# Attention inside a fused layer on one core: maxima from all parts of q and k, and a new order of TensorE's queue

## What is computed

```python
q = rope((x @ Wq.T + bq).reshape(B, L, H, hd))
k = rope((x @ Wk.T + bk).reshape(B, L, H, hd))
scores = einsum('bqhd,bkhd->bhqk', q, k) / sqrt(hd)
attn = softmax(scores)
out = einsum('bhqk,bkhd->bqhd', attn, v) @ Wo.T + bo
```

## Time and profile before

| | us |
|---|---|
| median of 3 runs | 5264.52 (5264.1 to 5265.49) |
| profiled execution | 5257.78 |
| its span, first to last instruction | 5255.9 |
| PE busy | 4717.2 (90%) |
| DVE busy | 3750.7 (71%) |
| POOL busy | 2560.1 (49%) |
| ACT busy | 2358.7 (45%) |

### The profile page before, as it was taken

One profiled execution on the slowest core, in us unless ns is written; L12 is line 12 of the kernel. 1 busy time (PEld: TensorE's weight loads), 2 busy tenths in 40 slices (PEclk: granted clock), 3 DMA queues, 4 the chain that ended last, 5 costly groups with the idle time before them and its releaser, 6 DMA issues. The chain is left out here.

```text
span 5255.9 us, 83572 instructions
## 1 busy us (share of the span) xinstructions
PE 4717.2 (90%) x25792; PEld 3011.7 (57%) x25792; DVE 3750.7 (71%) x5321; ACT 2358.7 (45%) x3683; POOL 2560.1 (49%) x1341
## 2 busy tenths in 40 slices
PE   6689999968888799999999999999996775999999
PEld 6678888846666433333333333333333664888888
DVE  6667777667787677777777777777774886677776
ACT  4433333322222255565656556565653343333332
POOL 2334444345565455555555555555554554344443
PEclk9999999989999799999999999999997886999999
DMA  4465555334444422222222232222214554555552
GB/s 136 139 198 179 172 176 161 119 135 159 153 144 140 133 51 64 63 64 64 64 58 57 63 64 64 62 64 64 64 37 129 169 160 139 177 178 168 173 175 91
DMA packets 431929, 613.85 MB, mean 117 GB/s; under 512 B 188288, under 2 KB 189568, under 8 KB 431808
## 3 DMA queue, kind: packets, MB, share of 16 engines
q1 hardware_dynamic: 390848, 545.67, 36.8%
q0 software_dynamic: 40960, 66.65, 4.0%
HBM read 452.44 MB, written 178.33 MB: 120 GB/s over the span
## 5 line engine op out<-in xcount | busy, mean ns | idle before, releaser
L1468 POOL TENSOR_TENSOR att_pairsum<-att_p,att_p 128x1024 f32<-128x1024 f32 x512 | 1203.1, 2369 | 994.5 <-ACT att_p L1486 994.5
L1540 DVE TENSOR_REDUCE att_halves<-att_mx 128x2 f32<-128x1024 f32 x1024 | 1211.2, 1221 | 534.3 <-PE att_mx L1579 531.1
L1486 ACT ACTIVATE att_p<-att_st 128x512 f32<-128x512 f32 x2048 | 1183.5, 597 | 869.1 <-PE att_st L1601 831.2
L1601 PE MATMUL att_st<-att_q,att_k 128*128 128x512 f32 x2048 | 960.3, 494 | 48.0 <-ACT att_p L1486 46.5
L1601 PEld LDWEIGHTS att_st<-att_q,att_k 128*128 128x128 f32 x2048 | 372.7, 187 | 825.7 <-issue 409.3
L1611 PE MATMUL att_op<-att_p,att_v 128*32 128x512 f32 x4096 | 549.0, 608 | 1.1 <-ACT att_p L1486 1.0
L1579 PE MATMUL att_mx<-att_k,att_q 32*128 32x512 f32 x2048 | 520.0, 503 | 27.7 <-DMA att_v<-v 15.1
L845 DVE TENSOR_TENSOR e_w<-e_raw,e_w 128x2048 fp32r<-128x2048 f32 x192 | 439.3, 2290 | 10.0 <-ACT e_w L840 6.1
L863 ACT ACTIVATE e_sg<-e_gp 128x324 f32<-128x324 f32 x256 | 113.3, 443 | 630.9 <-PE e_up L176 630.9
L840 ACT ACTIVATE e_w<-e_raw 128x2048 fp32r<-128x2048 f32 x192 | 366.4, 1909 | 56.1 <-DMA e_raw<-in_w_gate 48.1
L899 DVE SCALAR_TENSOR_TENSOR e_xg<-e_yp,e_meta,e_xg 108x512 f32<-108x512 f32 x192 | 144.2, 751 | 314.9 <-PE e_yp L176 314.9
(11 more groups left out here) (147 smaller groups left out, 9176.0 us busy)
## 6 DMA issues: line engine op xcount, KB each, us to landing
e_raw<-in_w_gate SPq DMA_DIRECT2D x64, 1024.0 KB, 5.6
e_raw<-in_w_up SPq DMA_DIRECT2D x64, 1024.0 KB, 9.5
e_raw<-in_w_down SPq DMA_DIRECT2D x64, 1024.0 KB, 5.8
att_q<-q SPq DMA_DIRECT2D x192, 256.0 KB, 4.1
att_k<-k SPq DMA_DIRECT2D x256, 128.0 KB, 5.8
r_x<-in_x SPq DMA_DIRECT2D x16, 1024.0 KB, 6.0
x<-r_base SPq DMA_DIRECT2D x16, 1024.0 KB, 9.4
qkv_x<-x SPq DMA_DIRECT2D x16, 1024.0 KB, 5.6
```

What stands on the lines that cost most here:

```text
L1468: nc.gpsimd.tensor_tensor(out=pairsum[h][g % 2][:, :], in0=pr[h][2 * g % RING][:, :], in1=pr[h][(2 * g + 1) % RING][:, :], op=ALU.add).the ...
L1486: nc.scalar.activation(pr[h][kt % RING][:, c * HALF:(c + 1) * HALF], st[c][:, :], ACT.Exp, scale=SCALE).then_inc(s_exp, 1)
L1540: nc.vector.tensor_reduce(out=halves[:, n // 2, n % 2, :], in_=mx[n % 2][:, :, :], axis=AX.X, op=ALU.max).then_inc(s_max, 1)
L1601: nc.tensor.matmul(st[c][:, :], kst[b][:, h, kt * P:(kt + 1) * P], qst[b][:, h, c * HALF:(c + 1) * HALF], start=True, stop=True).then_inc( ...
```

## The change

- `kst` is loaded as three blocks of both heads (parts 0, 1, 0), so `N_IN` is 7 and not 9.
- `rough` uses rows 0 to 96, all three terms of the product, one matmul for each head.
- Every step now has two roughs, one before each of its last two scores, and its first two scores follow each other. `TURN` is 3: from step 3 on the roughs are those of the pair after the next, ten of which are so made ahead (`FIRST` = 5 query tiles of two).
- The row is placed in step 4 (`ROW`) before the scores, into the bank of the sums `zp`, one 32-partition tile for each head and half. Each engine copies it in two halves.
- The totals of a pair's first two groups move from steps 4 and 6 to steps 5 and 6; the first waits for the copies of the row. `copy_z` moves from after score (3, 0) to after score (2, 2).
- DVE's split has two maxima of the same halves, one written in float32 and one in bfloat16, in place of a maximum and a cast. It comes after the reductions of step 2.

```diff
-    ROUGH = ((1, 1, 1), (1, 0, 1), (1, 1, 1), (1, 0, 1), (1, 1, 1), (0, 0, 0), (0, 0, 1), (1, 0, 1))
-    TURN = KT - 2
+    TURN = 3
+    ROW = TURN + 1
+    FIRST = KT - TURN
...
-                sp.dma_start(kst[b][2 * HD:3 * HD, :, :].bitcast(F32),
-                             k_in[0, src[0], :].rearrange("(h d) q -> d h q", h=2)).then_inc(s_in[b], 16)
-                for h in range(2):
-                    for blk in range(2):
-                        sp.dma_start(kst[b][blk * HD:(blk + 1) * HD, h, :].bitcast(F32),
-                                     k_in[KBLK[h][blk], bass.ds(p * (2 * HD) + h * HD, HD), :]).then_inc(s_in[b], 16)
+                for blk, part in enumerate((0, 1, 0)):
+                    sp.dma_start(kst[b][blk * HD:(blk + 1) * HD, :, :].bitcast(F32),
+                                 k_in[part, src[0], :].rearrange("(h d) q -> d h q", h=2)).then_inc(s_in[b], 16)
...
             def copy_row(i, b):
 
                 act.wait_ge(s_row, DEPTH * i + b + 1)
-                nc.scalar.activation(qst[b][3 * HD:4 * HD, 1, :],
-                                     mx[1][2 * HD:3 * HD, :, :].rearrange("p c q -> p (c q)"),
-                                     ACT.Copy).then_inc(s_rowq[1], 1)
+                for c in range(2):
+                    nc.scalar.activation(qst[b][3 * HD:4 * HD, 1, half(c)], zp[tile(1, c), :],
+                                         ACT.Copy).then_inc(s_rowq[1], 1)
...
-                        if last and (kt, x) == (3, 0):
+                        if last and (kt, x) == (2, 2):
                             copy_z(*last)
-                        if left and (kt, x) == (TURN, 3):
+                        if left and (kt, x) == (ROW, 2):
                             copy_row(*ahead(i, b, 1))
...
+            def split(i, b):
+
+                p = DEPTH * i + b
+                dve.wait_ge(s_max, 2 * KT * (p + 1))
+                dve.wait_ge(s_mlo, p)
+                nc.vector.tensor_tensor(out=big[:, :, :], in0=halves[:, 0, :, :], in1=halves[:, 1, :, :],
                                         op=ALU.max).then_inc(s_big, 1)
-                dve.wait_ge(s_big, p + 1)
-                nc.vector.tensor_copy(parts[:, :, :, 0], big[:, :, :]).then_inc(s_mhi, 1)
-                dve.wait_ge(s_mhi, p + 1)
+                dve.wait_ge(s_row, p)
+                nc.vector.tensor_tensor(out=parts[:, :, :, 0], in0=halves[:, 0, :, :], in1=halves[:, 1, :, :],
+                                        op=ALU.max).then_inc(s_big, 1)
+                dve.wait_ge(s_big, 2 * (p + 1))
                 nc.vector.tensor_tensor(out=parts[:, :, :, 1], in0=big[:, :, :], in1=parts[:, :, :, 0],
                                         op=ALU.subtract).then_inc(s_mlo, 1)
...
             def step(i, b, left):
                 if left:
-                    maxima(*ahead(i, b, 1))
-
-            maxima(0, 0)
+                    for qt in range(FIRST, KT):
+                        maxima(*ahead(i, b, 1), qt)
+                    split(*ahead(i, b, 1))
+                for qt in range(FIRST):
+                    if left >= 2:
+                        maxima(*ahead(i, b, 2), qt)
+                    if left and qt == ROW - TURN - 1:
+                        copy_row(*ahead(i, b, 1))
...
+                for h in range(2):
+                    last = nc.tensor.matmul(mx[c][:, h, :], qst[b][0:3 * HD, h, qt * P:(qt + 1) * P],
+                                            kst[b][0:3 * HD, h, half(c)], start=True, stop=True)
+                last.then_inc(s_mx, 1)
+
+            def row(i, b):
+
+                p = DEPTH * i + b
+                pe.wait_ge(s_mlo, p + 1)
+                pe.wait_ge(s_zo, past(p - 1))
+                for t in range(KT // 2):
                     for h in range(2):
...
+                        for c in range(2):
+                            last = nc.tensor.matmul(zp[tile(h, c), t * P:(t + 1) * P], parts[:, h, c * (KT // 2) + t, :],
+                                                    identb[:, :], start=True, stop=True)
                 last.then_inc(s_row, 1)
...
-                    if kt in (4, 6):
-                        totals(p, kt // 2 - 2)
-                    if kt == TURN:
-                        n = 0
-                    for part in range(4):
-                        if part < 2:
-                            scores(p, b, kt, 2 + part)
-                        elif kt + 1 < KT:
-                            scores(p, b, kt + 1, part - 2)
+                        totals(p - 1, 2 + kt // 2, left)
+                    if kt == ROW and left:
+                        row(*nxt)
+                    if kt in (ROW + 1, ROW + 2):
+                        totals(p, kt - ROW - 1, left)
+                    for x in (2, 3):
+                        scores(p, b, kt, x)
+                    for x in (0, 1):
+                        if kt < TURN and left:
+                            rough(*nxt, FIRST + kt, x)
+                        if kt >= TURN and left >= 2:
+                            rough(*ahead(i, b, 2), kt - TURN, x)
+                        if kt + 1 < KT:
+                            scores(p, b, kt + 1, x)
                         elif left:
-                            scores(p + 1, nxt[1], 0, part - 2)
...
+                            scores(p + 1, nxt[1], 0, x)
```

More of the change, by code:

```diff
@@ L1397, in attention, with tile, half @@
         N_OUT = 4
-        N_IN = 3 + 5 + 1
-        KBLK = ((0, 1, 0), (1, 0, 0))
+        N_IN = 3 + 3 + 1
+        def tile(h, c):
+            return slice((2 * h + c) * HD, (2 * h + c + 1) * HD)
+        def half(c):
+            return slice(c * HALF, (c + 1) * HALF)
         def ahead(i, b, k):
@@ L1533, in _, with maxima @@
             nc.vector.tensor_copy(identb[:, :], ident[:, :]).then_inc(s_identb, 1)
-            def maxima(i, b):
+            def maxima(i, b, qt):
                 p = DEPTH * i + b
[L1538 to L1544, removed]
+                for c in range(2):
+                    dve.wait_ge(s_mx, 2 * (KT * p + qt) + c + 1)
+                    if qt == 0 and c == 0:
+                        dve.wait_ge(s_big, 2 * p)
+                    nc.vector.tensor_reduce(out=halves[:, c, :, qt], in_=mx[c][:, :, :], axis=AX.X,
+                                            op=ALU.max).then_inc(s_max, 1)
@@ L1560, in _ @@
+            for qt in range(KT):
+                maxima(0, 0, qt)
+            split(0, 0)
+            copy_row(0, 0)
+            for qt in range(FIRST):
+                maxima(0, 1, qt)
             rounds_by(DEPTH, dve, NP, step)
@@ L1566, in _, with rough @@
             pe.wait_ge(s_identb, 1)
-            def rough(i, b, n):
+            def rough(i, b, qt, c):
                 p = DEPTH * i + b
-                qt, c = n // 2, n % 2
-                if n == 0:
+                if qt == 0 and c == 0:
                     pe.wait_ge(s_in[b], 16 * N_IN * (i + 1))
[L1574 to L1577, removed]
+                pe.wait_ge(s_max, past(2 * (KT * p + qt) + c - 1))
                 for h in range(2):
-                    last = nc.tensor.matmul(mx[n % 2][:, h, :], qst[b][h * HD:(h + 1) * HD, h, qt * P:(qt + 1) * P],
-                                            kst[b][h * HD:(h + 1) * HD, h, c * HALF:(c + 1) * HALF],
-                                            start=True, stop=True)
+                    last = nc.tensor.matmul(mx[c][:, h, :], qst[b][0:3 * HD, h, qt * P:(qt + 1) * P],
+                                            kst[b][0:3 * HD, h, half(c)], start=True, stop=True)
                 last.then_inc(s_mx, 1)
@@ L1586, in row @@
                 p = DEPTH * i + b
-                pe.wait_ge(s_max, NM * (p + 1))
                 pe.wait_ge(s_mlo, p + 1)
-                for qt in range(KT):
+                pe.wait_ge(s_zo, past(p - 1))
+                for t in range(KT // 2):
                     for h in range(2):
-                        last = nc.tensor.matmul(
-                            mx[1][(3 - h) * HD:(4 - h) * HD, qt // (KT // 2), qt % (KT // 2) * P:(qt % (KT // 2) + 1) * P],
-                            parts[:, h, qt, :], identb[:, :], start=True, stop=True)
+                        for c in range(2):
+                            last = nc.tensor.matmul(zp[tile(h, c), t * P:(t + 1) * P], parts[:, h, c * (KT // 2) + t, :],
+                                                    identb[:, :], start=True, stop=True)
                 last.then_inc(s_row, 1)
@@ L1610, in products, with totals @@
                     for c in range(2):
-                        last = nc.tensor.matmul(op[(2 * h + c) * HD:(2 * h + c + 1) * HD, :], v[b][:, kt, h, :],
-                                                pr[h][kt % RING][:, c * HALF:(c + 1) * HALF],
+                        last = nc.tensor.matmul(op[tile(h, c), :], v[b][:, kt, h, :], pr[h][kt % RING][:, half(c)],
                                                 start=kt == 0, stop=kt == KT - 1)
                 last.then_inc(s_v, 1)
-            def totals(p, g):
```

(25 more changed lines are left out.)

24 lines of the change are left out of this document (10 added, 14 removed).

## The result

The changed kernel takes 5288.07 us (median of 7 runs, 5278.68 to 5293.52), the kernel before in the same measurement 5263.24 (7 runs): ratio 1.0047, 95% interval 1.0036 to 1.0059. It is slower by 0.47%, or 25 us; the forecast was 5290. Its profiled execution took 5291.72 us, with a span of 5289.8.

The account below looks back on a forecast made before the run. PE's queue was taken to set the period of 33.73 us. Longer periods (21 us) and prologue (8), less 1 for the last but one pair, gave 28 us over the median 5264.52, rounded down to 5290; range 5268 to 5325.

Parts of the forecast that it names:

- The slots: Each step, u from its first score: chained matmuls start 0.23 us apart; plain step 3.41, with totals 4.27, with copies 4.44.
- rival 3: In the steps: the stall stands but slots are shorter, 0.05 us a step; about 5267 us; chance 0.11.
- Rival 2: On PE, chained matmuls of different tiles cost 0.34 us each or more: 2.7 us a period, 5460 us; chance 0.12.
- Step 4: Before the row, PE waits 1.7 us for DVE's split, which needs both POOL sums over; step 6.42 us, period 34.07.
- rival 1: DVE's split gets SBUF before POOL, so the row goes 1.74 us earlier; period 32.33 us, 5185 us; chance 0.23.
- The main part: In the steady state, each period is 0.34 us longer than before: 21 us over 62 periods.
- The prologue: Before the first score, seven more roughs of pair 1 are reduced, 1.13 us each: 8 us, bounds 0 and 16.
- The first and the last pairs: In the last but one pair, five steps lack roughs and are 0.3 us shorter: -1 us in the sum.

Follow-up runs that it names:

- e3: The changed kernel with both maxima of the split made by a reduction of one SBUF input: 5145.83 us, ratio 0.9784 to the kernel before.
- e7: The changed kernel with two matmuls of no use put in front of the row's wait to keep PE busy: 5246.88 us, ratio 0.9976 to the kernel before.
- e4: The changed kernel with the old rough products of 32 rows and the old loads of k: 5425.71 us, ratio 1.0317 to the kernel before.
- e2: The changed kernel with the split one step later and the row in step 5: 5145.32 us, ratio 0.978 to the kernel before.

## Why the prediction was right, and where two of its terms were not

**The slots.** Confirmed to 0.02 us up to the last score: in the step at 2513.68 the rough comes at u = 0.57, the next score at 1.18, rough 1 at 1.52, the last score at 1.99. From there to the products I took 0.43, a change of shape; it measured 0.33. Steps are thus 3.31 to 3.32 and 4.17 us, not 3.41 and 4.27, except those with a copy on ACT, which sets their last score: 4.44 and 4.45, as forecast. This is rival 3's cause at 0.1 us a step. Rival 2 is out: the scores' and roughs' chain runs at 0.23.

**Step 4.** Right in mechanism and size. From the first score of step 2 (2525.60): POOL at 3.38 (forecast 3.46), the split at 3.65 (3.63), the row at 8.49 (8.62), the step 6.37 (6.42). The row to its next score took 0.34, not 0.45, and the last score waited 0.33 for ACT. From the start of step 4's products to the row it is 2.58 us (2.62), which the profile shows as 1.51 idle because it counts the products' drain as busy. The lead of POOL that rival 1 hung on is 0.27. Rival 1 was priced too small, too: had the split been fast, as in e3, the period would have been 31.93 and not 32.33, since the steps are shorter than I had them.

**The clock: the term that I left out.** I read the wait of 1.7 us before the row as 1.7 us and nothing more. It also brings a half-speed stretch soon after in more than half of the periods, 37 us by e7. My rows had a steady period at 1.00 with idle times up to 0.56 us, and the first pair at 0.50; none had an idle time of this length in a steady period, and I gave the step from the one to the other no bound, though the first pair shows what half clock is like.

**The sum.** The main part was forecast at +0.34 a period and measured 34.15 - 33.78 = +0.37, so +23 us and not +21; but it is the sum of two errors that nearly cancel, -0.42 a period for the shorter steps and row (33.65, e7's mean, against 34.07) and +0.50 for the dips. (The first hides no error of the mechanism: it is 0.1 in each of the five steps without ACT's copies and 0.05 in step 4, less about 0.1 for the longer periods that e7 has as well.) The prologue took 11 us more, not 8: from the first rough to the first score 24.2 us before and 35.2 after. The clock is 0.50 there, and with two matmuls of 96 rows to a rough the roughs come 1.27 us apart (four in 5.08), where they came 1.13 apart before: 7 more of them are 8.9, and the other 19 are dearer by 0.14 each, 2.7, about 11 in all. I had priced the seven at DVE's pace and the others at nothing. The first and the last pairs gave back 8 us, not 1. Together 26 us against 28. The forecast's closeness is so in part luck: without the dips 5250 would have been the result, faster than before by what e7 shows and below the forecast's own range (5268 to 5325), and my chance for a gain of that kind (0.25) was put on another mechanism.

**What stays open.** Why a dip lasts 3.4 us in one period and 6.8 in another, and why 21 of the 56 steady periods have none at the same idle time, no run here shows.

## What to carry to other kernels

An operation of 0.2 us on DVE can take 2 us beside POOL's adds: here a maximum of two inputs in SBUF did, and a cast of one, and a reduction did not. Look at when POOL reads, or try another form of the operation, before moving its consumer around. A reordering should be costed with the stall that it creates and with what the stall does to TensorE's clock afterwards: a dip is seen only in the windows after the wait, and filling the gap with two matmuls that nobody reads got 37 us back. And when the order of a queue is tuned, remove one wait and read again: stall (140 us), ACT's copies (103) and the place of one rough (82) came into view one after the other.

## What the hardware did that I had not expected

- The granted clock fell to 0.50 *after* PE had resumed from an idle time of 1.5 to 1.6 us, in steady periods of the changed kernel 1.1 to 1.5 us after, for 3.4 or 6.8 us, in 35 of 56. e4, with waits of 1.1 to 1.4 us there, had dips in 53 of 56. With waits of at most 0.58 us (before), 0.5 (e7) or 0.9 (e2) the clock stayed at 1.00 from 1900 to 3600 us.
- Eight more matmuls a pair took the instruction queue from 65 to 183 packets and stopped PE for 3.0 to 3.5 us once per four pairs; two more did neither.
- A cast with one input in SBUF waited for POOL's sums as a maximum with two did (2.31 us against 0.20 before the first sum); a reduction did not (0.19 and 0.22 beside them, e3).
- A row on four column tiles is done in 0.34 us to the next score, against 0.55 on two; and a score that ends a chain in one shape is followed by the products after 0.33, one that comes by itself after 0.43.
